# Attention with mixture of experts: reciprocals of the softmax sums for two heads at once, the root of the first normalisation moved behind two scaled heads

## The reference

```python
def _L0_xattn_ref(q, k, v, mask, wq, bq, wk, bk, wv, bv, wo, bo):
    qh = proj(q, wq, bq); kh = proj(k, wk, bk); vh = proj(v, wv, bv)   # 16 heads of 32
    scores = jnp.einsum('bhqd,bhkd->bhqk', qh, kh) * scale
    scores = jnp.where(mask[None, None, :, :], scores, -1000000000.0)
    probs = jax.nn.softmax(scores, axis=-1)
    out = jnp.einsum('bhqk,bhkd->bhqd', probs, vh)
    return out.transpose(0, 2, 1, 3).reshape(b, s, d) @ wo.T + bo
...
x = x + _L0_xattn_ref(_layernorm(x), ctx, ctx, mask, ...)     # x, ctx: (32, 256, 512) f32
x = x + _L0_ffn_ref(_layernorm(x), w_gate, c_fc, c_proj)      # 8 experts, top 2
```

## Time and profile before

| | |
|---|---|
| median of 3 runs | 2894.36 us (2890.72 to 2902.14) |
| profiled execution, its own time | 2905.15 us |
| its span | 2903.3 us |
| busy share of the span: PE, PEld, DVE, ACT, POOL | 97%, 78%, 55%, 47%, 44% |
| reciprocals L775 | 512, 160 ns median |
| scaling products L427 | 1024, mean 508 ns |

### The profile page before, as it was taken

The page is one execution under the profiler, slowest core; times in us unless marked ns, Lnnn a source line. Parts: engine busy times, 40 slices in busy tenths (PEclk is TensorE's granted clock), DMA queues, the critical chain, the costliest instruction groups (busy, mean ns, idle before and its releaser), DMA issues.

```text
span 2903.3 us, 53159 instructions
## 1 busy us (share of the span) xinstructions
PE 2802.2 (97%) x17472; PEld 2267.8 (78%) x17472; DVE 1589.4 (55%) x5156; ACT 1372.3 (47%) x3628; POOL 1275.6 (44%) x1920
## 2 busy tenths in 40 slices
PE   7999999999999999959999999999999999999997
PEld 5777777777777777737888888888888888888886
DVE  6878888888888888853333242333332332423331
ACT  5767767677777777733233232232332322323221
POOL 5667777777777777652122222222221212121211
PEclk9999999999999999979999999999999999999999
DMA  4355444444444444435343444434443434343312
GB/s 147 107 111 132 129 123 128 109 121 125 123 132 127 129 126 125 107 91 147 90 89 90 84 99 82 100 80 95 88 95 80 103 77 99 83 85 93 74 29 29
DMA packets 247367, 296.30 MB, mean 102 GB/s; under 512 B 40384, under 2 KB 159168, under 8 KB 245568
## 3 DMA queue, kind: packets, MB, share of 16 engines
q1 hardware_dynamic: 184032, 159.58, 21.3%
q0 software_dynamic: 32768, 67.26, 13.3%
q10 hardware_dynamic: 30304, 66.07, 6.9%
HBM read 125.26 MB, written 67.90 MB: 67 GB/s over the span
## 4 chain that ended last, share of the span: by engine, by line
PE 53%; DMA 1%; issue 0%; ACT 0%; SPq 0%; POOL 0%; DVE 0%; POOLq 0%
PE a_ps L1658 18%; PE g_ps L1658 18%; PE y_ps L1673 18%; DMA out<-y,recs 0%; DMA fc_raw<-in_c_fc 0%; ACT fc_hi L1514 0%; POOL out L1499 0%; ACT L1554 0%; SPq L1393 0%; DVE hidden L1621 0%; ACT y L1570 0%; ACT act_part L1554 0%; SPq L1388 0%; POOLq L69 0%; SPq L69 0%
## 5 line engine op out<-in xcount | busy, mean ns | idle before, releaser
L1499 POOL DMA_INDIRECT out<-y,recs x128 | 205.5, 1606 | 1183.8 <-ACT y L1570 854.1
L427 POOL TENSOR_SCALAR probs<-probs,row_inv 128x256 f32<-128x256 f32 x1024 | 504.2, 508 | 284.8 <-DVE row_inv L775 270.7
L1621 DVE TENSOR_TENSOR hidden<-act_part,g_ps 128x512 f32<-128x512 f32 x192 | 132.0, 687 | 894.0 <-ACT act_part L1554 894.0
L570 ACT ACTIVATE probs<-probs,low 128x256 f32<-128x256 f32 x1024 | 510.3, 501 | 226.8 <-DVE low L766 174.8
L766 DVE CUSTOM_DVE_ANT_0 probs<-scores_ps,mask_add,row_any 128x256 f32<-128x256 f32 x1024 | 429.1, 474 | 13.1 <-remote 8.8
L1658 PE MATMUL a_ps<-xe_hi,fc_hi 128*128 128x512 f32 x768 | 299.8, 390 | 4.6 <-DVE xe_lo L1577 2.6
L1673 PE MATMUL y_ps<-pj_hi,ht_hi 128*128 128x512 f32 x768 | 299.5, 390 | 0.7
L1658 PE MATMUL a_ps<-xe_lo,fc_hi 128*128 128x512 f32 x768 | 299.2, 390 | 0.0
L1658 PE MATMUL a_ps<-xe_hi,fc_lo 128*128 128x512 f32 x768 | 299.2, 390 | 0.0
L1673 PE MATMUL y_ps<-pj_hi,ht_lo 128*128 128x512 f32 x768 | 298.9, 389 | 0.0
L1673 PE MATMUL y_ps<-pj_lo,ht_hi 128*128 128x512 f32 x768 | 298.8, 389 | 0.0
(11 more groups left out here) (204 smaller groups left out, 6456.2 us busy)
## 6 DMA issues: line engine op xcount, KB each, us to landing
probs_m<-blocks SPq DMA_DIRECT2D x1024, 64.0 KB
x_quarters<-xg SPq DMA_DIRECT2D x496, 64.0 KB
fc_raw<-in_c_fc SPq DMA_DIRECT2D x24, 1024.0 KB, 5.8
out<-x_xn ACTq DMA_DIRECT2D x32, 512.0 KB, 2.8
xn_rows<-x_xn ACTq DMA_DIRECT2D x32, 512.0 KB
cin<-in_ctx_t ACTq DMA_DIRECT2D x31, 512.0 KB, 6.1
xin<-in_x ACTq DMA_DIRECT2D x31, 512.0 KB, 4.4
quarters<-xn_rows SPq DMA_DIRECT2D x120, 128.0 KB
```

What stands on the lines that cost most here:

```text
L427: last = nc.gpsimd.tensor_scalar(probs[:, r, t, :], probs[:, r, t, :], row_inv[:, r, t:t + 1], 1.0, ALU.mult, ALU.mult)
L570: last = nc.scalar.activation(probs[:, r, t, :], probs[:, r, t, :], ACT.Exp, scale=-1.0, bias=low[:, r, t:t + 1], accum_out=row_sum[:, r, ...
L1499: nc.gpsimd.indirect_dma_start(out=out[:, :], out_offset=bass.IndirectOffsetOnAxis(ap=recs[:, i * CT + t, 0:1].bitcast(U32), axis=0), in_= ...
L1621: nc.vector.tensor_tensor(hidden[:, m % 2, :], act_part[:, m % 2, :], g_ps[m % 2][:, :], ALU.mult).then_inc(gated, 1)
```

## The change

The reciprocals are taken for two heads by one instruction (128x4 in place of 128x2), which waits until both heads' exponents are done. The first pair of a group is inverted behind all four masks of the group, the second pair where head 3 was inverted before. POOL's root of the first normalisation comes behind two scaled heads of group 0, not three.

```diff
@@ gpsimd step
                         if has(n):
-                            for r in range(2 if c == 3 else 3):
+                            for r in range(2 if c in (0, 3) else 3):
                                 scale(g + r)
                         if c == 0 and has(n + 1) and n >= 0:
                             root(0, n + 1, ln1_var, ln1_chain, ln1_rstd, xn_ready)
...
                         if has(n):
-                            for r in range(2 if c == 3 else 3, HPC):
+                            for r in range(2 if c in (0, 3) else 3, HPC):
                                 scale(g + r)
@@ vector
                 def invert(g):
+
                     r = g % RING
-                    dve.wait_ge(exped, g + 1)
-                    nc.vector.reciprocal(row_inv[:, r, :], row_sum[:, r, :]).then_inc(inverted, 1)
+                    dve.wait_ge(exped, g + 2)
+                    nc.vector.reciprocal(row_inv[:, r:r + 2, :], row_sum[:, r:r + 2, :]).then_inc(inverted, 2)
...
                         for r in range(HPC):
                             mask_scores(g * HPC + r)
-                            if r >= 2:
-                                invert(g * HPC + r - 2)
+                        invert(g * HPC)
...
                     if proj and n >= 0:
                         moments_x(n + 1)
-                    if heads:
-                        invert(g * HPC + 2)
                     if has(n - 3):
                         record(n - 3)
                     if heads:
-                        invert(g * HPC + 3)
+                        invert(g * HPC + 2)
```

More of the change, by code:

```diff
@@ L940, in step @@
                         attn_lo(g - 1)
-                    if heads:
-                        invert(g * HPC + HPC + 2)
                     if proj and n >= 0:
@@ L945, in step @@
                     if heads:
-                        invert(g * HPC + HPC + 3)
+                        invert(g * HPC + HPC + 2)
                     if late:
@@ L955, in step @@
                         x2_out(n - 1, 0)
-                    if heads:
-                        invert(g * HPC + 2 * HPC + 2)
                     if late:
@@ L961, in step @@
                     if heads:
-                        invert(g * HPC + 2 * HPC + 3)
+                        invert(g * HPC + 2 * HPC + 2)
                     if tail:
@@ L974, in step @@
                         attn_lo(g + 1)
-                    if heads:
-                        invert(g * HPC + 3 * HPC + 2)
                     if late:
@@ L979, in step @@
                     if heads:
-                        invert(g * HPC + 3 * HPC + 3)
+                        invert(g * HPC + 3 * HPC + 2)
                     if n == LAST:
```

## The result

| | before | changed |
|---|---|---|
| median, us | 2897.69 (2890.72 to 2902.14, 4 runs) | 2945.52 (2945.2 to 2948.42, 4 runs) |
| ratio, 95% interval | | 1.0174 [1.0159, 1.0189] |
| span of the profiled execution, us | 2903.3 | 2943.9 |
| step (turn of group 2 to the next), median of 31, us | 38.28 | 39.91 |
| reciprocals of softmax sums | 512 | 256 |

The change is slower by 1.74%; 1.5% was forecast. The two profiled executions are only 40.6 us apart, the medians 47.8: the profile of the kernel before was slower than all of its four timed runs, and four of its 31 steps took 45.8, 42.0, 39.8 and 39.7 us. In the two longest PE stood idle for 5.6 and 2.0 us, and its granted clock was down to 0.57 between 170 and 175 us and to 0.74 between 520 and 525 us. The step medians leave these out: they differ by 1.63 us.

What follows compares the result with a forecast made beforehand. PE, 97% busy, was held by a chain over POOL's scaling, DVE's turn and masks, and ACT's exponents. Terms of 30.1, 9.3 and 3.1 us made 42.5 us, 2936.9 us from the 2894.36 median; range 2908 to 2956.

Steps and rivals of the forecast that it cites:

- At both places PE has no slack: Before a step's first `score` (0.40 us wait) and first `probs_turn` (0.46 us): later queries' copy or mask delays PE equally.
- Term A: Group 2: both last heads' products fall behind the pair's reciprocal, so the turn comes 0.94 us later each step.
- The wait of the pair for head 3's exponents is no new cost: Group 2 on DVE: head 3's reciprocal already waited for the same thing at the same place, so nothing is added.
- Term B: Group 3: heads 0 and 1 scaled later, delaying the second normalisation's root and group 0's masks by 0.31 us a step.
- Term C: Group 0: root 0.70 us earlier but turn 0.63 us later, mostly absorbed; 0.1 us a step passes on.
- ACT then idles 0.44 us for PE's transposes: After group 1's exponents: this idling of ACT absorbs most of the 0.63 us lateness of group 0's turn.
- The sum: Whole kernel: 30.1, 9.3 and 3.1 us make 42.5 us; 2936.9 us from the median, 1.5% slower.
- Two blocked parts of: Rival, group 0: POOL waits for both parts of `normalise_x`, turn 1.04 us late, 15.5 us more, 2952 us; chance 0.12.
- for one of the two instructions: Group 0: head 3's 0.43 us loss beside `normalise_x` fits DVE's exclusion of POOL for one 0.55 us part, not both.
- Only A counts: Rival: moments set group 3's root and group 0's lateness is absorbed, leaving group 2's 30.1 us: 2924.5 us; chance 0.11.
- Nothing moves: Rival: PE's queries and ACT's copy could be late anyway, so group 2's delay meets an existing gap: 2894 us; chance 0.12.
- Faster: Rival: POOL catches up, turns don't wait for the last pair, 0.64 us a step leaves PE's chain: 2874.5 us; chance 0.08.

Runs made afterwards that it cites:

- Shortening the chain by itself: Kernel before with moved root and earlier statistics of x2's first half: -10.7 us; with queries' copy and normalise_x2 also earlier: -9.0 us.
- the parts measured alone: Kernel before with single edits: group 2's heads 2 and 3 paired +31.1 us; group 0's pairs and moved root +19.9; group 3's heads 0 and 1 paired +9.8.
- three pairs cost no position on the chain: Kernel before with shared reciprocals for group 1's first pair, group 2's first and group 3's last: +1.9 us, ratio 1.0007.

## Why the prediction was right, and which term was too small

- *The bound.* "At both places PE has no slack" held: PE's gap before `score` grew from 0.40 to 1.19 us and before the first `probs_turn` from 0.46 to 0.77; 1.3 and 0.8 were forecast. The 0.40 us was more than the usual 0.23; on the average of the stretch the wait grew by 0.95 us. Shortening the chain by itself also shortened the step.
- *Term A*, forecast 0.94 us: 0.91 in the trace (2.22 less 1.31), 0.97 alone (31.1 / 32). "The wait of the pair for head 3's exponents is no new cost" was off by the 0.07 us told above.
- *Term B*, forecast 0.31: 0.32 in the trace, 0.33 alone.
- *Term C*, forecast 0.1: this is the term that was mis-sized. The turn of group 0 was 0.56 us late of its own, near the 0.63 forecast, but the step "ACT then idles 0.44 us for PE's transposes" was taken as cover for nearly all of it. In the trace of the changed kernel the copy of x starts late all the same, and PE stands at the output projection behind ACT's copy of the keys:

```profile
604.95 0.58 ACT L499 CAST xt_hi<-bank_a 128x512 fp32r<-128x512 f32 x1 [0.26 <-PE bank_a L1021]
```
```profile
607.30 0.19 PEld L1078 LDWEIGHTS bank_b<-w_hi,at_hi 128*128 128x128 f32 x1 [0.31 <-ACT qk L538]
```

  From the turn of group 2 the copy starts at 26.22 us, before at 25.59: 0.63 later, 0.31 beyond B (0.22 by the medians of 30 steps). The wait of 0.44 us became one of 0.26, it didn't vanish, because the time at which PE's semaphore ended it moved too: 1.78 us behind the start of the transposes in this step, 1.47 in the one of before. The forecast took that end as fixed. On the other chips there is no such wait, and C is 0.58 us.
- *The sum.* 32 x 0.91, 30 x 0.32 and 31 x 0.31 give 48.3 us; 47.8 were measured. The forecast had 42.5; the difference is C. That the sum is so near is partly luck: C is read from one step, the four runs of the kernel before lie over 11 us, and the step medians grew by 1.63 us where the three terms make 1.54.
- *Two blocked parts of* `normalise_x`: the four products beside it took 0.33 us more than others, where this rival had 0.84. Two of them took 0.65 and 0.64 us and the other two 0.47, and the second part of `normalise_x` took 0.71 us where the first took 0.55, so POOL was not kept out for both parts; the prediction's agreement "for one of the two instructions" rests on the size of the loss alone. "Only A counts" and "Nothing moves" are excluded by the parts measured alone.
- *Faster.* Sound in one half that was not counted: the moved root alone gains 5.5 us. The saved reciprocals gain nothing: where three pairs cost no position on the chain, the time is that of before.

## What to carry to other kernels

A small instruction that releases a queue behind it is worth its position and not its duration: merging two of them makes the first consumer wait for the second producer, and where the consumer's queue was using that time, its whole work (here 0.94 us of products for 0.08 us of reciprocal) moves behind the last release. Merge where the consumer is late anyway, and look what its shifted work then runs beside. When a wait is to serve as cover, ask what ends it: that can move with the change, or be missing where the kernel runs next.

## What the runs showed of the hardware

- One program took 2897.7 us in the first runs and 2876 to 2877 us on three other chips, 0.7% less. In the traces PE's semaphore behind the transposes of x comes 1.37 us after their start in the first and 0.61 us in the others; an edit's cost differed with it (47.8 and 59.8 us). Whether the chip or something else in the first runs makes this is open.
- GpSimd's products lengthen VectorE's small routing operations beside them: a cast of 128x4 took up to 0.49 us beside a product and at most 0.17 where none ran, in the first trace of the changed kernel with a median of 0.42 us. The Trainium skill (SBUF — State Buffer, Who interferes with whom) has this as a lock of the shared port for a whole instruction. The traces agree in size, since the cast lost at most 0.33 us and a product takes 0.47; most casts beside a product took 0.16 us, and that the lock is the cause is not shown.
- A reciprocal of 128x4 took 0.16 to 0.18 us, one of 128x2 0.13 to 0.17, over all traces: four values cost nearly what two do.
